# Projections of queries, keys and values as three fp32r products of two exact parts

## What is computed

```python
x = x + attn(layernorm(x))
x = x + ffn(layernorm(x))

def attn(x):                                                  # in fp32
    q, k, v = x @ Wq.T + bq, x @ Wk.T + bk, x @ Wv.T + bv     # 256 x 256 each
    q, k = rope(q), rope(k)
    out = softmax(q @ k.T / 4) @ v                            # per head
    return out @ Wo.T + bo

def ffn(x):
    xc = x.astype(bfloat16)
    normed = rmsnorm(xc) * norm_weight
    w = softmax of the two largest of 8 logits, 0 elsewhere
    p1 = normed @ mlp1[e]; g, lin = min(p1[0::2], 7), clip(p1[1::2], -7, 7)
    p2 = (g * sigmoid(1.702 * g) * (lin + 1)) @ mlp2[e]
    return xc + sum over e of w[e] * p2
```

## Time and profile before

| | |
|---|---|
| time, median of 3 runs | 1128.25 us (1126.47 to 1128.8) |
| the profiled execution | 1125.54 us, its span 1123.7 us |
| PE busy | 953.0 us, 85% of the span |
| DVE busy | 822.6 us, 73% |
| ACT busy | 694.7 us, 62% |
| POOL busy | 427.2 us, 38% |
| mean granted PE clock | 0.938 of full speed |

### The profile page before, as it was taken

One profiled execution on the slowest core, in us unless ns is written; L12 is line 12 of the kernel. 1 busy time (PEld: TensorE's weight loads), 2 busy tenths in 40 slices (PEclk: granted clock), 3 DMA queues, 4 the chain that ended last, 5 costly groups with the idle time before them and its releaser, 6 DMA issues.

```text
span 1123.7 us, 16639 instructions
## 1 busy us (share of the span) xinstructions
PE 953.0 (85%) x5288; PEld 400.6 (36%) x5288; DVE 822.6 (73%) x1641; ACT 694.7 (62%) x905; POOL 427.2 (38%) x356
## 2 busy tenths in 40 slices
PE   4629999889888998989989898989999999995564
PEld 1302222234342443334442343324443443343343
DVE  5751211589968898589958898588968996997897
ACT  2317887766657675766658575766668777760231
POOL 2413302534364334543354434543342332333242
PEclk9868999999999999999999999999999999996686
DMA  5353434344545244444534244444534454331110
GB/s 162 97 120 69 114 82 115 81 104 110 114 90 137 72 105 109 109 101 103 124 82 117 82 108 106 104 91 114 124 82 114 105 123 97 89 91 38 42 57 24
DMA packets 79987, 109.81 MB, mean 98 GB/s; under 512 B 22530, under 2 KB 56722, under 8 KB 76818
## 3 DMA queue, kind: packets, MB, share of 16 engines
q1 hardware_dynamic: 61460, 83.47, 32.5%
q10 hardware_dynamic: 18432, 25.17, 7.7%
HBM read 82.90 MB, written 25.69 MB: 97 GB/s over the span
## 4 chain that ended last, share of the span: by engine, by line
PE 49%; DVE 27%; issue 8%; ACT 6%; POOL 3%; DMA 3%; SPq 2%; ACTq 0%; DVEq 0%; POOLq 0%
PE OP L698 14%; PE S L684 13%; PE D L670 7%; ACT probs L815 4%; DVE act_sb L1123 4%; DVE th_sb L1118 4%; DVE acc L1113 3%; PE A L653 3%; DVE l_sb L1103 3%; PE D L574 3%; DVE g_sb L1101 3%; PE BB L653 3%; PE D L596 3%; DMA o_scr<-O 1%; PE D L588 1%
## 5 line engine op out<-in xcount | busy, mean ns | idle before, releaser
L815 ACT ACTIVATE probs<-S 128x1024 f32<-128x1024 f32 x512 | 511.4, 1022 | 200.4 <-PE S L684 196.7
L684 PE MATMUL S<-Qs,Ks 98*128 98x512 bf16 x1024 | 304.2, 390 | 30.3 <-DMA Qs<-m_scr 15.2
L698 PE MATMUL OP<-probs,V 128*17 128x512 f32 x2048 | 276.4, 612 | 3.0 <-ACT O L824 3.0
L899 POOL TENSOR_TENSOR act_lo<-act_sb,act_hi 128x512 fp32r<-128x512 f32 x128 | 166.3, 1300 | 197.3 <-DVE act_hi L1129 160.8
L684 PEld LDWEIGHTS S<-Qs,Ks 98*128 98x128 bf16 x1024 | 80.3, 99 | 213.8 <-ACT probs L815 95.0
L670 PE MATMUL D<-W,act_hi 128*128 128x256 f32 x448 | 131.6, 326 | 14.0 <-DVE Vn L997 5.8
L1113 DVE SCALAR_TENSOR_TENSOR acc<-D,combh,acc 128x256 f32<-128x256 f32 x224 | 97.1, 475 | 45.8 <-PE D L670 45.6
L1118 DVE SCALAR_TENSOR_TENSOR th_sb<-th_sb,g_sb 128x512 f32<-128x512 f32 x128 | 126.8, 991 | 0.2
L893 POOL TENSOR_SCALAR W<-W2b 128x512 fp32r<-128x512 bf16 x64 | 46.1, 720 | 204.8 <-PE D L670 199.7
L670 PE MATMUL D<-W,act_lo 128*128 128x256 f32 x448 | 112.7, 284 | 0.0
L1123 DVE SCALAR_TENSOR_TENSOR act_sb<-l_sb,th_sb 128x512 f32<-128x512 f32 x128 | 106.0, 828 | 4.4
(11 more groups left out here) (138 smaller groups left out, 991.7 us busy)
## 6 DMA issues: line engine op xcount, KB each, us to landing
W<-in_w ACTq DMA_DIRECT2D x64, 256.0 KB, 2.9
Ks<-k_scr SPq DMA_DIRECT2D x32, 384.0 KB
W2b<-in_w ACTq DMA_DIRECT2D x64, 128.0 KB, 3.1
Ks<-k_scr SPq DMA_DIRECT2D x32, 256.0 KB
o_scr<-O SPq DMA_DIRECT2D x32, 256.0 KB, 4.7
q_scr<-parts SPq DMA_DIRECT2D x16, 384.0 KB, 3.5
k_scr<-parts SPq DMA_DIRECT2D x16, 384.0 KB, 2.5
Qs<-q_scr SPq DMA_DIRECT2D x32, 192.0 KB
```

The lines of the kernel that those rows point to most:

```text
L684: last = mm(S[:, j2, C * i:C * (i + 1)], Ks[0:SROWS + MROWS, g % 2, j, P * kt:P * (kt + 1)], Qs[0:SROWS + MROWS, g % 2, j, :], start=True, ...
L698: last = mm(OP[32 * j:32 * j + VW, :], V[:, kt, HG * g + j, :], probs[:, s % 2, C * j:C * (j + 1)], start=kt == 0, stop=kt == KT - 1)
L815: nc.scalar.activation(probs[:, s % 2, 2 * C * j2:2 * C * (j2 + 1)], S[:, j2, :], ACT.Exp, scale=SCALE).then_inc(exp_done, 1)
L899: tt(act_lo[:, e % 2, it, :], act_sb[:, a % 2, :], act_hi[:, e % 2, it, :].bitcast(FP32), ALU.subtract).then_inc(lo_s, 1)
```

## The change

Weights and transposed input are each held as two fp32r tiles: the value rounded to fp32r (`wqk_h`, `wv_h`, `xnT_h`) and the rest (`wqk_l`, `wv_l`, `xnT_l`). A projection is the sum of high x high, high x low and low x high: three fp32r matmuls where one fp32 matmul stood.

The weights are split once, in the head, by a new stage `split`: ACT copies (rounds), POOL subtracts, and PE waits for `w_lo` ahead of the first `qk` and the first `v`. The transposed input is split in each unit: ACT copies both halves out of the bank, DVE subtracts each copy from the bank, and only then is the bank free.

To make room, some tiles are shared: the fp32 weights are loaded into `probs`, `xn` is written over `X` (so the load of the next X waits for the transposes, and unit 1 of the head is loaded into `X1s`), `Mt` lies in `sw`, `x2b` in `nf`, and the zeros for `m_scr` come from `act_sb`. `xT1` moves by one half step, from 8 to 9, and `x_next` from 8 to 12.

```diff
-    AT = {"x_next": 8, ..., "xT0": 7, "xT1": 8,
+    AT = {"x_next": 12, ..., "xT0": 7, "xT1": 9,
...
-    HEAD = [..., ("early", 0, 0), ("xT", 0, 0), ("xT", 1, 0)]
+    HEAD = [..., ("early", 0, 0), ("split", 0, 0), ("xT", 0, 0), ("xT", 1, 0)]
...
         if i == 1:
-            HEAD += [("xn", 0, 1), ("x_next", 0, 1)]
+            HEAD += [("xn", 0, 1)]
         if i == 2:
-            HEAD += [("weights", 0, 0)]
+            HEAD += [("weights", 0, 0), ("split", 1, 0)]
...
+        if i == 4:
+            HEAD += [("x_next", 0, 1)]
...
-        xn = sb("xn", [P, TC, E], FP32)
-        xnT = sb("xnT", [P, CT, C], FP32)
+        xn = X
+        xnT_h, xnT_l = sb("xnT_h", [P, CT, C], FP32R), sb("xnT_l", [P, CT, C], FP32R)
...
+        wqk_sb = probs[:, 0, 0:CT * 2 * E].rearrange("p (c n) -> p c n", c=CT)
+        wv_sb = probs[:, 1, 0:CT * E].rearrange("p (c n) -> p c n", c=CT)
...
+                elif st == "x_next" and u + 1 < B * NCH:
+
+                    sp.wait_ge(xnT_s, 2 * (u + 1))
+                    sp.dma_start(x_of(u + 1), x_v[bass.ds(u + 1, 1)].rearrange("o p t c -> (o p) t c")).then_inc(x_ld, 16)
...
                 elif st == "qk":
 
+                    if u == 0 and a == 0:
+                        pe.wait_ge(w_lo, 1)
                     pe.wait_ge(xnT_s, 2 * (u + 1))
                     for c in range(CT):
-                        last = mm(bank[:, :], wqk_sb[:, c, P * a:P * (a + 1)], xnT[:, c, :], start=c == 0, stop=c == CT - 1)
+                        for i, (w, xt) in enumerate(((wqk_h, xnT_h), (wqk_h, xnT_l), (wqk_l, xnT_h))):
+                            last = mm(bank[:, :], w[:, c, P * a:P * (a + 1)], xt[:, c, :],
+                                      start=c == 0 and i == 0, stop=c == CT - 1 and i == 2)
...
                 elif st == "v":
+                    if u == 0 and a == 0:
+                        pe.wait_ge(w_lo, 2)
                     for t in range(2):
+                        tok = P * (2 * a + t)
                         for c in range(CT):
-                            last = mm(bank[:, E * t:E * (t + 1)], xnT[:, c, P * (2 * a + t):P * (2 * a + t + 1)], wv_sb[:, c, :],
-                                      start=c == 0, stop=c == CT - 1)
+                            for i, (xt, w) in enumerate(((xnT_h, wv_h), (xnT_h, wv_l), (xnT_l, wv_h))):
+                                last = mm(bank[:, E * t:E * (t + 1)], xt[:, c, tok:tok + P], w[:, c, :],
+                                          start=c == 0 and i == 0, stop=c == CT - 1 and i == 2)
...
-                if st == "xT" and a == 0:
+                if st == "split":
+                    act.wait_ge(*((c_late, 16 * N_LATE) if a else (c_ld, 16 * N_LOADS)))
+                    full, high = ((wqk_sb, wqk_h), (wv_sb, wv_h))[a]
+                    nc.scalar.copy(high[:, :, :], full[:, :, :]).then_inc(w_hi, 1)
+                elif st == "xT":
                     act.wait_ge(d_full, k + 1)
-                    nc.scalar.copy(xnT[:, 0, :], bank[:, :]).then_inc(xnT_s, 1)
+                    nc.scalar.copy(xnT_h[:, a, :], bank[:, :]).then_inc(xnT_hs, 1)
...
+                elif st == "split":
+                    if a:
+                        pool.wait_ge(c_late, 16 * N_LATE)
+                    full, high, low = ((wqk_sb, wqk_h, wqk_l), (wv_sb, wv_h, wv_l))[a]
+                    pool.wait_ge(w_hi, a + 1)
+                    tt(low[:, :, :], full[:, :, :], high[:, :, :].bitcast(FP32), ALU.subtract).then_inc(w_lo, 1)
...
-                    v.memset(Mt[:, :, :], 0.0).then_inc(c_set2, 1)
+                    v.memset(act_sb[:, :, :], 0.0).then_inc(c_set2, 1)
...
-                elif st == "xT" and a == 1:
-                    dve.wait_ge(d_full, k + 1)
-                    v.tensor_copy(xnT[:, 1, :], bank[:, :]).then_inc(xnT_s, 1)
+                elif st == "xT":
+                    dve.wait_ge(xnT_hs, 2 * u + a + 1)
+                    v.tensor_tensor(xnT_l[:, a, :], bank[:, :], xnT_h[:, a, :].bitcast(FP32), ALU.subtract).then_inc(xnT_s, 1)
                 elif st == "rope":
+                    if n == 0 and bb and a < 2:
+                        dve.wait_ge(m_w, 16 * bb)
...
                 elif st == "nf":
                     dve.wait_ge(rrms_s, u + 1)
+                    if u:
+                        dve.wait_ge(x2_s, 2 * u)
...
+                    if n < 2:
+                        dve.wait_ge(m_zero, 16 * B)
```

More of the change, by code:

```diff
@@ L43, in block_kernel @@
                  out, safe_score=SAFE_SCORE):
-    AT = {"x_next": 8, "stats1": 1, "rstd1": 1, "xn": 4, "xT0": 7, "xT1": 8, "qk0": 10, "qk1": 12, "qk2": 22,
+    AT = {"x_next": 12, "stats1": 1, "rstd1": 1, "xn": 4, "xT0": 7, "xT1": 9, "qk0": 10, "qk1": 12, "qk2": 22,
           "qk3": 30, "rope": 2, "part1": 3, "length": 5, "part2": 7, "part3": 10, "v0": 37, "v1": 42, "gmax": 1,
@@ L102, in block_kernel @@
         l.sort(key=lambda e: (ORDER.index(e[0]), e[1]))
-    HEAD = [("stats1", 0, 0), ("rstd1", 0, 0), ("xn", 0, 0), ("x_in", 0, 1), ("early", 0, 0), ("xT", 0, 0), ("xT", 1, 0)]
+    HEAD = [("stats1", 0, 0), ("rstd1", 0, 0), ("xn", 0, 0), ("x_in", 0, 1), ("early", 0, 0), ("split", 0, 0), ("xT", 0, 0), ("xT", 1, 0)]
     for i in range(4 * NCH + 2):
@@ L195, in block_kernel @@
         rec_scr = scratch("rec_scr", (B * NCH, NG, HG, C), FP32)
-        wqk_sb = sb("wqk_sb", [P, CT, 2 * E], FP32)
+        wqk_h, wqk_l = sb("wqk_h", [P, CT, 2 * E], FP32R), sb("wqk_l", [P, CT, 2 * E], FP32R)
         bqk_sb = sb("bqk_sb", [P, 4], FP32)
-        wv_sb = sb("wv_sb", [P, CT, E], FP32)
+        wv_h, wv_l = sb("wv_h", [P, CT, E], FP32R), sb("wv_l", [P, CT, E], FP32R)
         bv_sb = sb("bv_sb", [P, E], FP32)
@@ L240, in block_kernel @@
         rec_c = sb("rec_c", [P, 16], FP32)
-        Mt = sb("Mt", [H, MROWS, L], BF16)
+        Mt = sw[0:H, :, :].bitcast(BF16)
         mx = sb("mx", [P, TT, H], FP32)
@@ L247, in block_kernel @@
         nf = sb("nf", [P, TC, E], BF16)
-        x2b = sb("x2b", [P, TC, E], BF16)
+        x2b = nf
         nfT = sb("nfT", [P, CT, C], BF16)
@@ L286, in block_kernel @@
         D = ps("D", [P, C], FP32)
+        w_hi, w_lo, xnT_hs = sem("w_hi"), sem("w_lo"), sem("xnT_hs")
         c_ld, c_late, c_set, c_set2, passed = (sem(n) for n in ("c_ld", "c_late", "c_set", "c_set2", "passed"))
@@ L322, in block_kernel, with x_of @@
         out_v = out.rearrange("b (n t p) c -> (b n) p t c", p=P, t=TC)
+        def x_of(u):
+            return X1s[:, 1, :, :] if in_head(u) and u else X[:, :, :]
         def bank_of(filling):
@@ L436, in stage @@
                     for i in range(B):
[L437 to L443, removed]
+                        sp.dma_start(m_scr[i].rearrange("r h t -> h r t"), act_sb[0:H, :, :].bitcast(BF16)).then_inc(m_zero, 16)
+                elif st == "x_in":
+                    to = x_of(u)
+                    if u:
+                        sp.wait_ge(stat1, TC * u)
+                    sp.dma_start(to, x_v[bass.ds(u, 1)].rearrange("o p t c -> (o p) t c")).then_inc(x_ld, 16)
+                elif st == "x_next" and u + 1 < B * NCH:
+                    sp.wait_ge(xnT_s, 2 * (u + 1))
+                    sp.dma_start(x_of(u + 1), x_v[bass.ds(u + 1, 1)].rearrange("o p t c -> (o p) t c")).then_inc(x_ld, 16)
                 elif st == "part3":
@@ L949, in stage @@
                     dve.wait_ge(x_ld, 16 * (u + 1))
-                    norm_stats(X, st1, mv1, var1, stat1, aggr1, var1_s, u)
+                    norm_stats(x_of(u), st1, mv1, var1, stat1, aggr1, var1_s, u)
                 elif st == "xn":
                     dve.wait_ge(rstd1_s, u + 1)
+                    source = x_of(u)
+                    if u == 1:
+                        dve.wait_ge(xnT_s, 2)
                     for t in range(TC):
-                        v.tensor_scalar(xn[:, t, :], X[:, t, :], mv1[:, t, 0:1], rstd1[:, t:t + 1],
+                        v.tensor_scalar(xn[:, t, :], source[:, t, :], mv1[:, t, 0:1], rstd1[:, t:t + 1],
                                         ALU.subtract, ALU.mult).then_inc(xn_s, 1)
-                elif st == "xT" and a == 1:
-                    dve.wait_ge(d_full, k + 1)
-                    v.tensor_copy(xnT[:, 1, :], bank[:, :]).then_inc(xnT_s, 1)
+                elif st == "xT":
+                    dve.wait_ge(xnT_hs, 2 * u + a + 1)
+                    v.tensor_tensor(xnT_l[:, a, :], bank[:, :], xnT_h[:, a, :].bitcast(FP32), ALU.subtract).then_inc(xnT_s, 1)
                 elif st == "rope":
+                    if n == 0 and bb and a < 2:
+                        dve.wait_ge(m_w, 16 * bb)
                     wait_apart(dve, (qk_b, 4 * u + a + 1), *([(qk_p3, 4 * u + a - 1)] if looped(u) or u or a >= 2 else []))
```

## The result

The changed kernel takes 1152.8 us (median, 1150.47 to 1154.7), the kernel before 1128.53 on the same chip: a ratio of 1.0218 with a 95% interval of 1.0192 to 1.0244, some 24 us slower. The forecast was 1127.1, the range ended at 1134. The profiled execution of after took 1150.47, its span is 1148.6; before 1125.54 and 1123.7.

A forecast was written before the change was run, and what follows sets the result against it. The prediction took a chain shared by PE and DVE, with bank D's turn, as the bound. Head +3.55 and loop -4.65 gave -1.1 us, so 1127.1 us; range 1118 to 1134.

The forecast's parts named there:

- What bounds it, the choice of stages: In the loop's full units, qk0 to qk2 and v0 count in the chain; qk3 and v1 are covered by DVE.
- The price of a product: Projections: fp32r matmul of 512 columns 0.215 us; qk stage 1.72 to 1.30, v stage gains 0.23.
- The rival of the dear product: Projections: fp32r matmul costs 0.43 like fp32, so a qk stage takes 2.6 and the kernel 1143 us; chance 0.05.
- The turn of the bank, +0.75: Full units 4 to 7: bank D is held longer, so qk0 starts 0.65 to 0.85 us late, taken as 0.75.
- the part of qk2 and v0, 0.65: Full units: shorter qk2 saves 0.42 and shorter v0 0.23 us in the chain.
- Units 2 and 3, -1.65: First two loop units: unit 2 gains 1.0 us net, unit 3 gains 0.65 by qk2 and v0.
- The head, +3.55 with bounds 2.3 to 4.8: First 66 us: first result 2.05 late, v stages and their transposes add 1.9, a shorter qk stage returns 0.4.
- The second split: Head: splitting the values' weights on POOL takes 1.3 us, ends at 32.4; v stages begin then, not at 29.00.
- The sum: Whole kernel: head 3.55 less loop 4.65 gives -1.1 us, so 1127.1 against the median.
- the rival of the longer turn: Units 2 and 4 to 7: longer bank waits lower PE's clock, +4 to +10 us, about 1134; chance 0.20.
- The sign that I had named for it: Loop units: a granted PE clock well below 1 between the transposes and qk1 would show the lower clock.
- The cashed saving: Loop: all 24 qk and 12 v stages count, 12.8 us less the head, 9.3 gained, so 1119; chance 0.25.

The follow-up runs named there:

- the kernel with 64: The changed kernel plus 64 never-executed instructions in PE's untaken branch at the first turn: 1136.44 us, ratio to before 1.0087.
- The trace without the jump: The changed kernel with the exact path, which these inputs never take, left out of PE's program: 1137.47 us, 1.0086 of before.
- the two kernels without gaps: The changed kernel with 64 never-executed instructions added in PE's untaken branch (1136.44 us), and with PE's exact path left out (1137.47 us).
- 256: The changed kernel plus 256 never-executed instructions, a whole block, in PE's untaken branch at the first turn: 1156.59 us in one execution.
- 208: The changed kernel plus 208 never-executed instructions in PE's untaken branch at the first turn: 1151.17 us.
- before with 128 idle instructions: The kernel before the change plus 128 never-executed instructions in PE's untaken branch at the first turn: 1138.71 us, 1.0118 of before.
- the kernel with one product: The changed kernel with 64 never-executed instructions added, leaving out two of the three products of each projection: 1133.52 us in one execution.
- the head that was mended: On the changed kernel with 64 never-executed instructions added: DVE rounds the first weights, values' weights split before the third rotation; 1133.44 us in one execution.

## Why the prediction was wrong, point by point

**What bounds it, the choice of stages:** right as a map, wrong as a price list. PE's share of the chain is not what a shorter PE gives back: 34 us less work in the loop brought at most some 7, of which 4.6 by their trace came in the head.

**The price of a product:** right. In the chain of the kernel with 64:

```profile
605.38 1.40 PE D L592 x6
...
635.28 1.59 PE D L611 x12
```

1.40 was forecast as 1.30, 1.59 as 1.71, for 1.72 and 1.94 in the earlier trace rows. The six start 0.23 apart, near the 0.215. The rival of the dear product falls.

**The turn of the bank, +0.75:** this term was mis-sized in the loop. In unit 4, whose rows I took the earlier trace rows, it holds: the first subtraction, forecast at 312.14, came at 312.1 in the old time (317.05 less 4.9), down product 12 at 314.9 (forecast 315.1), qk0 0.85 late. But its second transposes took 1.11 where those of unit 5 took 0.85, with the clock on its way up: in before the bank turned faster in unit 5, by 0.6, and the change adds 1.5 there. I had taken one unit for four. From the first transposes to qk0 units 4 to 7 took 7.1, 6.5, 7.1 and 6.5 us in before, 7.8, 8.0, 8.3 and 8.0 with 64: 0.7 to 1.5 more each. qk0 itself went from 1.98 to 1.67, a gain of 0.31 for the 0.42. By the exponentials units 4 to 7 cost 1.2, 0.2, 0.1 and 0.0 us with 64, for a forecast gain of 0.75 each; the part of qk2 and v0, 0.65, came about as forecast. The trace without the jump, which has no gap either, is dearer: 1.2, 1.8, 1.0 and 3.0.

**Units 2 and 3, -1.65:** -2.85 in after, -1.1 and -2.4 in the two kernels without gaps, 0.0 and -2.7 in those with 256 and 208, which have none so early: right within their spread.

**The head, +3.55 with bounds 2.3 to 4.8:** 4.5 in after, step by step a little over. The first result was late by 2.46 (2.05 forecast). The second split stood where I had put it, ahead of POOL's subtraction of the earlier trace rows, so v0 came 6.0 late, the 3.4 and that delay. qk0 of unit 1 came 4.7 late, 2.25 more than the first result (1.9 forecast). But after is the mildest of six traces with this head: in the others the first exponential is 5.5 to 6.8 late, over my upper bound. Part of that is loads that landed up to 0.7 later; before with 128 idle instructions is itself late by 0.7.

**The sum:** -1.1 became +7.4 without the gaps in the profiled execution of the kernel with 64 (1132.94 for 1125.54): 4.4 by the four full units, 2.4 by the head (with loads that landed later), 0.6 by units 2 and 3, and 0.8 behind the last projections, where before with 128 lost 2.2 too. That was the fastest of six executions; by the medians it is 10 (7 to 13), and with the gaps 24. For the gaps the sum has no term at all. That is the step that failed: I costed each matmul that the change adds by its time, and none by its place in PE's program. The runs showed in its place two waits of PE for its own instructions, 6.69 and 7.50 us, and the lower clock behind them. The page has the 47 blocks of instructions, and the kernel a branch over more than a block at each turn; but no turn of before waits, so neither the price nor the ends of the blocks could be read there. That the change met two of the three turns is chance: 64 idle instructions more, and it meets none.

**The rivals.** The clock (the rival of the longer turn): it fell where I had named it, in some of the units: at qk0 of unit 6 in after (2.58 us at a granted 0.58, for 1.67), of units 4 and 7 without the jump (2.91 and 2.44), of unit 4 in the kernel with 64. There two of qk0's matmuls start 0.42 apart, twice the 0.23 of the first:

```profile
323.01 0.63 PE L592 MATMUL D<-xnT_h,wqk_h 128*128 128x512 f32 x1
...
323.43 0.63 PE L592 MATMUL D<-xnT_l,wqk_h 128*128 128x512 f32 x1
...
324.00:328.00 4.00, 4.00 (x22) 1.54 (x20) 0.14 (x1) 2.47 (x3) 1.28 (x1) 0.75 0.00 0
```

With 64 unit 4 lost 1.2 us; without the jump units 4 and 7 lost 1.2 and 3.0, so the low end of the +4 to +10 is not excluded for that trace. The sign that I had named for it can't tell: in before too the granted clock over the transposes of units 4 to 7 was 0.50 to 0.58. The cashed saving is refuted by the kernel with one product.

## What to carry to other kernels

If an edit changes the number of instructions ahead of a branch, count where the branch and its target lie in the blocks that the engine loads; a path that is never taken, unrolled to more than a block, makes the time a lottery of 7 us per turn, and a "same code, other place" copy of the kernel is the cheap test. A gap with no releaser at a branch, with one block of instructions landing in it, is what it looks like. And shortening an engine that shares the chain with another can be worth little, as here: cut its work to a third in one throw-away kernel before spending effort on two thirds.

## What the runs showed that was not expected

- PE waits 6.69 to 7.50 us at a branch that skips the next 16 KB block, 3.18 to 4.96 shortly behind a target near that block's end, and pays the lower clock behind it: 9 and 10 us by the exponentials.
- Rounding 1024 elements per partition took DVE 0.69 (in the head that was mended) and ACT 1.04; POOL's subtraction of as many took 2.35.
- DVE's cast of 128x512 takes 0.43 as a rule, and 2.47 started inside POOL's addition of 128x1024; three kernels differ from two by 3 us at that one place.
- Kernels that execute the same instructions stand 1.7 to 5.5 us behind before at the end of batch 0, ahead of any gap: a few us in one trace are no finding.
